# The value products of an attention pipeline in pairs, every second pass

## The reference

```
xl = layernorm(x)                      # 8 batches, 512 tokens, 128 features
q, k = xl @ W_qk ; v = xl @ W_v        # 8 heads, 64 features for q and k, 16 for v
dots = q k^T * 64**-0.5 + bias(head, clipped distance)
attn = softmax(dots) ; out = attn @ v
x = x + out @ W_out + b_out
```

## Time and profile before

| what | value |
|---|---|
| time, median of 3 runs | 1154.55 us (1154.54 to 1154.6) |
| the profiled execution's own time | 1156.07 us |
| its span, first to last instruction | 1154.2 us |
| attention stage in it | about 604 to 1059 us |
| PE, DVE, ACT, POOL busy over the span | 90%, 78%, 71%, 45% |
| DMA packets' mean rate | 78 GB/s |

### The profile page before, as it was taken

One profiled execution on the slowest core, in us unless ns is written; L12 is line 12 of the kernel. 1 busy time (PEld: TensorE's weight loads), 2 busy tenths in 40 slices (PEclk: granted clock), 3 DMA queues, 4 the chain that ended last, 5 costly groups with the idle time before them and its releaser, 6 DMA issues. The chain is left out here.

```text
span 1154.2 us, 23485 instructions
## 1 busy us (share of the span) xinstructions
PE 1035.0 (90%) x7816; PEld 797.0 (69%) x7816; DVE 896.2 (78%) x1941; ACT 823.9 (71%) x1736; POOL 516.6 (45%) x322
## 2 busy tenths in 40 slices
PE   4876699999999999979968999999999999987997
PEld 3443578999899899759965555555555555546897
DVE  7798998888889889856646778787878787785565
ACT  3997998898898988636645666676766676651665
POOL 0288898898998989634530001010101010111354
PEclk9997699999999999999989999999999999998999
DMA  3001265555786686333322000000000000001331
GB/s 98 4 3 40 69 154 141 133 155 140 192 253 163 180 217 170 92 97 107 95 76 60 1 1 19 1 19 1 20 1 19 1 20 1 20 20 61 108 97 51
DMA packets 107782, 89.50 MB, mean 78 GB/s; under 512 B 35815, under 2 KB 85740, under 8 KB 107664
## 3 DMA queue, kind: packets, MB, share of 16 engines
q1 hardware_dynamic: 98784, 66.02, 22.1%
q0 software_dynamic: 5568, 12.66, 3.1%
q10 hardware_dynamic: 3312, 9.33, 2.7%
HBM read 71.49 MB, written 17.39 MB: 77 GB/s over the span
## 5 line engine op out<-in xcount | busy, mean ns | idle before, releaser
L1084 DVE TENSOR_TENSOR_SCAN h<-d_a,p_dbu 128x1024 f32<-128x1024 f32 x128 | 289.7, 2279 | 30.4 <-ACT d_a L828 26.3
L770 POOL TENSOR_TENSOR h<-h,c_rep 128x1024 f32<-128x1024 f32 x126 | 297.6, 2391 | 22.1 <-DVE h L1084 20.8
L1412 POOL DMA_INDIRECT expert_rows<-r_row,r_dest x60 | 59.4, 991 | 447.5 <-DVEq L1307 432.8
L828 ACT ACTIVATE d_a<-arena,a_exp 128x511 f32<-128x511 f32 x256 | 167.9, 710 | 13.5 <-DVE h L1084 13.3
L2131 DVE CUSTOM_DVE_ANT_0 arena<-at_p_scores,arena 128x512 f32<-128x512 f32 x256 | 161.3, 686 | 19.0 <-PE at_p_scores L1934 17.2
L2140 DVE COPY at_probs_T<-at_p_probs_T 128x512 f32<-128x512 f32 x128 | 88.0, 687 | 72.8 <-PE at_p_probs_T L1942 72.1
L976 PE MATMUL p_y_T<-ident,h 128*128 128x128 f32 x1024 | 132.5, 273 | 1.2 <-DVE h L1139 1.1
L2047 ACT ACTIVATE at_probs<-arena,at_min 128x512 f32<-128x512 f32 x145 | 98.2, 712 | 47.0 <-DVE at_min L2131 47.0
L820 ACT ACTIVATE b_du_T<-arena,b_T 128x256 f32<-128x256 f32 x304 | 128.7, 495 | 0.0
L1934 PE MATMUL at_p_scores<-arena,at_q_T 64*128 64x512 f32 x512 | 127.2, 615 | 0.9 <-DVE arena L2123 0.9
L976 PEld LDWEIGHTS p_y_T<-ident,h 128*128 128x128 f32 x1024 | 115.9, 142 | 1.7 <-DVE h L1139 1.7
(11 more groups left out here) (272 smaller groups left out, 1767.6 us busy)
## 6 DMA issues: line engine op xcount, KB each, us to landing
c_rep<-c_rows SPq DMA_DIRECT2D x128, 256.0 KB
diag_b<-diag_rows SPq DMA_DIRECT2D x52, 256.0 KB
f_row<-expert_rows SPq DMA_DIRECT2D x78, 129.0 KB, 2.2
arena<-in_w_all ACTq DMA_DIRECT2D x8, 578.0 KB
arena<-bias_by_distance ACTq DMA_DIRECT2D x8, 448.0 KB
x_tok<-in_x SPq DMA_DIRECT2D x4, 512.0 KB, 5.7
x_tok<-x_between SPq DMA_DIRECT2D x8, 256.0 KB, 2.7
diag_rows<-diag_b SPq DMA_DIRECT2D x4, 256.0 KB, 3.0
```

The lines of the kernel that those rows point to most:

```text
L770: nc.gpsimd.tensor_tensor(h_at(n), h_at(n), cc, ALU.mult).then_inc(prod_done, 1)
L828: nc.scalar.activation(da[:, s % 2, ch, 1:], delta[:, one(b), ch, 1:].squeeze(1), ACT.Exp, scale=a_exp[:, ch, s:s + 1]).then_inc(da_ready, 1)
L1084: nc.vector.tensor_tensor_scan(h_at(n).rearrange("p c t -> p (c t)"), da[:, s % 2, :, :].rearrange("p c t -> p (c t)"), p_dbu[:, s % 2, :, ...
```

## The change

1. `values`: instead of one half group in each pass n >= 2, every odd pass n >= 3 makes both halves (`values(n-3)`, `values(n-2)`), and even passes make none.
2. V moves from slot A to slot B of pass 7, on PE and on ACT.
3. DVE: the part 0 of `norm(b, 0)` moves from ahead of the takes to between them in pass 5, part 1 to pass 6, part 2 to pass 7; in passes 6 and 7 `take(4n)` goes ahead of the fourth `bias`; `add_bias` moves behind the takes of pass 7.
4. Start: four dummy products fewer; the first two score products wait for q0 and k0 alone, the other two for q1 and k1.
5. End: the last group of values goes to a bank of `psc`, and normalising, output product and addition are made in two halves of 256 columns; the first half is normalised behind the takes of the last pass. Dummy products between: 2 instead of 9.

```
-        AT_A = {0: "X", 1: "k0", 2: "k1", 3: "q2", 4: "R", 5: "q3", 7: "V"}
-        AT_B = {0: "q0", 1: "q1", 2: "O", 3: "k2", 4: "L", 5: "N", 6: "k3"}
+        AT_A = {0: "X", 1: "k0", 2: "k1", 3: "q2", 4: "R", 5: "q3"}
+        AT_B = {0: "q0", 1: "q1", 2: "O", 3: "k2", 4: "L", 5: "N", 6: "k3", 7: "V"}
...
             def quad(n):
                 b, part = divmod(n, QUADS)
-                if part == 0:
-                    pe.wait_ge(proj_taken, taken(b, "q1" if b == 0 else "k1"))
-                    if b == 0:
-                        pe.wait_ge(first_k, 2)
+                if part == 0 and b > 0:
+                    pe.wait_ge(proj_taken, taken(b, "k1"))
...
                 for g in range(4 * n, 4 * n + 4):
...
+                    if g in (0, 2):
+                        pe.wait_ge(proj_taken, taken(0, "q0" if g == 0 else "q1"))
+                        pe.wait_ge(first_k, g // 2 + 1)
...
-            k.keep_busy(pot, 6)
+            k.keep_busy(pot, 2)
...
-                if n >= 2:
+                if n >= 3 and n % 2:
+                    values(n - 3)
                     values(n - 2)
...
+            def last_output(half):
+                pe.wait_ge(last_norm, 4 * half + 4)
+                for j in range(TPB // 2):
+                    at_t = (half * TPB // 2 + j) * P
+                    for gr in range(NG):
+                        mm = nc.tensor.matmul(last_out[half][:, j * P:(j + 1) * P], onT[gr][:, at_t:at_t + P],
+                                              w_o[:, gr, :], start=gr == 0, stop=gr == NG - 1)
+                mm.then_inc(o_half, 1)
+
+            pe.wait_ge(biased, ALL)
             for i in range(B * QUADS - 2, B * QUADS):
                 values(i)
-            pe.wait_ge(biased, ALL)
-            k.keep_busy(psc[:, 0, :], 9)
-            slot(B, "O")
+            use_bank(added, B)
+            pe.wait_ge(normed, B * NG - 1)
+            last_output(0)
+            k.keep_busy(psc[:, 0, :], 2)
+            last_output(1)
...
+            def last_normed(half):
...
+                dve.wait_ge(valued, 2 * n + 1 + half)
...
+                V.transpose(o_tok.rearrange("p n e -> p (n e)")[:, cols], last_sums[half]).then_inc(last_norm, 1)
...
-                elif part == 5:
-                    norm(b, 0, 0)
...
                 elif part == 5:
+                    norm(b, 0, 0)
+                elif part == 6:
                     norm(b, 0, 1)
-                elif part == 6:
+                elif part == 7:
                     norm(b, 0, 2)
-                elif part == 7 and b + 2 < B:
-                    add_bias(b + 2)
...
+                elif part == 7 and b + 2 < B:
+                    add_bias(b + 2)
+                elif part == 7 and b == B - 1:
+                    last_normed(0)
...
-                if n + 1 < B * QUADS:
-                    for g in range(4 * n + 4, 4 * n + 8):
+                more = n + 1 < B * QUADS
+                if more:
+                    for g in range(4 * n + 4, 4 * n + 7):
                         bias(g)
+                if part in (6, 7):
+                    take(4 * n)
+                if more:
+                    bias(4 * n + 7)
                 ahead_of_takes(b, part)
-                take(4 * n)
+                if part not in (6, 7):
+                    take(4 * n)
...
-            norm(B - 1, 1, 0, 1, 2)
-            add(B - 1)
+            last_normed(1)
+            last_add(0)
+            last_add(1)
```

More of the change, by code:

```diff
@@ L1807, in attention @@
         turned_taken = [S("turned_taken0"), S("turned_taken1")]
+        last_norm, o_half, half_added = S("last_norm"), S("o_half"), S("half_added")
         norm_step, normed, o_done, added = S("norm_step"), S("normed"), S("o_done"), S("added")
@@ L1825, in attention @@
         rt.veps, rt.rstd, rt.rstd_ready, rt.rstd_from = veps[:, 1, :], rstd[:, 1, :], rstd_ready, 3
+        LAST_VALUES = B * ST // VS - 1
+        HALF = T // 2
+        last_sums = [pot[:, 0:HALF], psc[:, 2, 0:HALF]]
+        last_out = [pmm[:, 0:HALF], psc[:, 1, 0:HALF]]
         LOGITS_READ, RANKS_READ = 12, 21
@@ L1959, in values @@
                     for q in range(HG):
-                        mm = nc.tensor.matmul(pot[32 * q:32 * q + 32, it * P:(it + 2) * P],
+                        dst = pot[32 * q:32 * q + 32, it * P:(it + 2) * P]
+                        if vg == LAST_VALUES:
+                            dst = psc[32 * q:32 * q + 32, 2, 0:HALF]
+                        mm = nc.tensor.matmul(dst,
                                               vv[b % 2][:, j, hd0 + q, :], prT[:, vg % 2, q, j, :],
@@ L2160, in norm, with last_add @@
                     V.transpose(onT[gr], o_norm).then_inc(normed, 1)
+            def last_normed(half):
+                n = B * NG - 1
+                cols, blocks = slice(half * HALF, (half + 1) * HALF), slice(half * HALF // 32, (half + 1) * HALF // 32)
+                dve.wait_ge(valued, 2 * n + 1 + half)
+                dve.wait_ge(norm_step, 2 * n)
+                V.transpose(o_tok.rearrange("p n e -> p (n e)")[:, cols], last_sums[half]).then_inc(last_norm, 1)
+                dve.wait_ge(last_norm, 4 * half + 1)
+                V.reciprocal(rden[:, blocks], o_tok[:, blocks, DV]).then_inc(last_norm, 1)
+                dve.wait_ge(last_norm, 4 * half + 2)
+                dve.wait_ge(normed, n)
+                V.tensor_tensor(o_normed[:, blocks, :], o_tok[:, blocks, :],
+                                rden[:, blocks].unsqueeze(2).to_broadcast([P, HALF // 32, 32]),
+                                ALU.mult).then_inc(last_norm, 1)
+                dve.wait_ge(last_norm, 4 * half + 3)
+                dve.wait_ge(o_done, B - 1)
+                V.transpose(onT[1][:, cols], o_norm[:, cols]).then_inc(last_norm, 1)
+            def last_add(half):
+                dve.wait_ge(o_half, half + 1)
+                dve.wait_ge(x_biased, B)
+                at_j = (B - 1) * TPB + half * TPB // 2
+                xb = k.x[:, at_j:at_j + TPB // 2, :]
+                V.tensor_tensor(xb, last_out[half].rearrange("p (j e) -> p j e", j=TPB // 2), xb,
+                                ALU.add).then_inc(added if half else half_added, 1)
             def add(b):
@@ L2228, in _ @@
             plan.make_pad(dve)
-            norm(B - 1, 1, 0, 1, 2)
-            add(B - 1)
+            last_normed(1)
+            last_add(0)
+            last_add(1)
+            dve.wait_ge(half_added, 1)
             route(B - 1, *range(0, 12))
```

## The result

| | before | after |
|---|---|---|
| median, us | 1154.57 (4 runs, 1154.54 to 1154.85) | 1166.47 (4 runs, 1165.53 to 1166.87) |
| ratio | 1 | 1.0107, 95% interval 1.0093 to 1.0122 |
| profiled execution: time, span, mean granted clock | 1156.07, 1154.2, 0.975 | 1166.5, 1164.5, 0.967 |

The kernel is 1.0 to 1.1% slower: the medians lie 11.9 us apart, which is 1.03%, and the ratio on record, which is not the quotient of the medians, is 1.0107. Forecast were 1156.8 us, 2.2 more than before, and a range that ended at 1163.0. The sign was right, the size was not.

A forecast was written before the change was run, and what follows sets the result against it. PE was taken to bound odd passes and a bias, exps and copy chain the even ones; 5.6 + 1.3 + 0.6 - 1.8 - 2.1 - 1.4 = +2.2 on 1154.55 us gave 1156.8, range 1154.0 to 1163.0.

The forecast's parts named there:

- rival C: Even passes leave PE idle 1 us or more, so the clock falls, 3 to 5 us each; chance 0.03.
- what stands outside the stage: Ahead of and behind the attention stage: forecast at 0 us in the sum.
- Odd passes bound by PE, even ones by bias, three exps and the copy of slot A: Passes 1, 3, 5, 7 change by +0.68, +0.62, +0.69, +0.29 us; passes 0, 2, 4, 6 by 0, -0.33, 0, -0.84.
- 0.86 for the second half group, not 1.00: In odd passes the joined second half of values adds 0.86 us, as one drain between groups goes.
- Pass 6, the early signal: In pass 6 PE's first two turns signal before the late stretch: 5.51 us (-0.84), or 6.35 (0) if held.
- Batch 7, start and end: Batch 7 -1.8 us; start of the stage -1.4 (bounds -0.4 and -1.5); end -2.1 (bounds -0 and -2.7).
- the 0.8 that I expected of its pass 6: Pass 6 of batch 7, which has no projections, gains 0.8 us, within that batch's estimate of -1.8.
- batches 1 to 5: The pass changes sum to +1.11 us for each of these five batches, +5.6 in all.
- the prediction's own sign of being wrong: Wrong if the granted clock falls within the stage, pass 0 comes under 6.2 us, or odd passes pass 7.7.
- The bound for "can tell" (0.2%): This kernel's measurement was taken to tell differences of about 0.2%, 2.3 us.

The follow-up runs named there:

- e4: The kernel before without the first half group of each pair of values, queries scaled by 0.01: 1157.34 us, against 1155.24 for before.
- e3: The kernel before, unchanged, run again on chip 1: 1155.58 us, ratio 1.0001.
- e11: The changed kernel with four dummy products ahead of slot B in pass 4 alone: 1160.89 us, ratio 1.0019 to the kernel before.
- e14: The changed kernel, unchanged, run again on chip 4: 1163.07 us, ratio 1.0072 to the kernel before.
- e2: The kernel before with only the start and end edits of the change: 1152.19 us, ratio 0.9975.
- e6: The changed kernel with one half group of values in every pass n >= 2 again, all other edits kept: 1151.39 us, ratio 0.9909 to before.
- e10: The kernel before with the router's sends of batches 0 to 5 held to run beside pass 0 of the next batch: 1161.83 us, ratio 1.0016.
- e12: The kernel of e6 with the router's sends held as in e10: 1152.15 us, ratio 0.9933 to the kernel before.
- e13: The changed kernel with values paired only in pass 7, none in pass 6, one half group in passes 0 to 5: 1149.18 us, ratio 0.9954 to before.
- e5: The changed kernel with eight dummy products ahead of slot B in passes 0 and 4 of each batch (not the first): 1167.88 us, ratio 1.0053 to before.
- e7: The changed kernel, unchanged, run again on chip 2: 1163.48 us, ratio 1.0007 to the kernel before.

## Why the prediction was wrong

Two terms that the sum had at nothing failed: the clock inside the stage (rival C, chance 0.03) took 3.29 us, and what stands outside the stage took 4.01 + 0.53 us in the compared execution (points 5 and 6). The mechanism of the passes held. Point by point:

1. *Odd passes bound by PE, even ones by bias, three exps and the copy of slot A.* Right, and shown by every trace of the change: where the clock held, the pass lengths came out within 0.1 us on four chips. e4 shows the even passes' half of it without any pairing.
2. *0.86 for the second half group, not 1.00.* Right: the odd passes carry it (7.52 forecast as 7.53). The 0.14 saved is nothing beside the 0.6 to 0.7 that passes 1, 3 and 5 lose each.
3. *Pass 6, the early signal.* Right, and worth 0.87 a batch against a before with late signals, 0.40 against one without. The size of the term changes with the chip or the execution, which the rows could not tell: before's pass 6 is 6.35, 5.89, 6.34 and 5.88 in its four profiles (the first comparison, chips 1, 3 and 4). The prediction's rule that signals due about 1.3 us or more behind the first send are seen late was read from one execution of before; in pass 6 of e3, with the same distances, nothing was late.
4. *Batch 7, start and end.* Batch 7's passes up to the last scores gave 36.72 - 37.59 = -0.87 without the clock (e11 against before); the 0.8 that I expected of its pass 6 falls by these landmarks into the end, which gave -2.61. Together -3.48, forecast -1.8 - 2.1 = -3.9. The start gave -0.71 in the first pair and -1.34 in e14 for -1.4. All of it, with the clock falls in the passes and what lies outside the stage taken out, is 10.33 - 3.29 - 4.01 - 0.53 = +2.5 us; the forecast was +2.2, and e11 measured +1.8. That it comes so near is partly luck: batches 1 to 5 cost 0.6 less than forecast and the start saved 0.7 less.
5. *"Rival C, the clock ... I give it little."* This is the step that failed within the stage, and the prediction's own sign of being wrong, a fall of the clock within it, came. I argued from pass 0 of batch 0, which held 1.00 with PE busy 5.35 of 6.37. Pass 4, just as empty in the table (5.33 of 6.49), is another thing: it is mostly transposes and small router products. In all six profiles of kernels without values in pass 4, and without a fill, low stretches lie at the end of pass 4 or in pass 5, one to five each; in no profile of before, e2, e6, e10, e12, e13, e5 or e11 does one. e5 and e11 differ from after by the fill alone, so the evidence is that the fall comes from what PE does not do in pass 4; it rests on one profile of each, and the falls without a fill are themselves irregular. One fall costs 1.5 to 1.7 us, not the 3 to 5 us that I had for it. The Trainium skill (TensorE: Matmul & The Clock Gate, "A second HAM failure mode: psum-queue depth-cycling") says of another kernel that the clock goes back and forth where the PE idles briefly and often between groups of matmuls; these runs agree in kind, but the clock fell about two of the eight passes 4 in the first profile, and about one of them in e7.
6. *The sum against one execution's time.* The other 4.01 us lay ahead of the stage, and 0.53 behind it. I took what is not changed to cost nothing, and in the mean it does: the sign of that term turned round on chip 4, and over all profiles x is loaded at 603.9 in the four of before and at 603.0 in the three of after. But one comparison carries it, and no bound of mine held it. The bound for "can tell" (0.2%) was too small likewise: before itself took 1154.6, 1155.2, 1163.2, 1159.1 and 1155.0 us in five comparisons, and after against before gave 1.0107, 1.0007 and 1.0072, or +11.9, +0.3 and +8.1 us between the medians. Their mean, +6.7, is near the +2.5 and 3.3 of point 4 and the clock together.

Open: why the copy on DVE took 4.71 us, and why all four runs of after in the first comparison were slow; how an indirect send holds back a signal of PE; and why pass 4 lets the clock fall and pass 0 does not. That pass 0 has a 512 column projection in its second slot is not the answer by itself, for pass 0 of batch 7 has no projection, makes PE wait 1.43 us where pass 4 of batches 1 to 7 makes it wait 1.15, and the clock held there in every profile. Pass 4 of batch 0, which has no router products, is as empty (PE busy 4.00 of 5.43) and never saw a fall either. Pass 0 of batch 7 in the first profile of the changed kernel:

```profile
1003.30:1008.74 5.44, 4.01 (x26) 2.40 (x25) 3.87 (x11) 3.97 (x7) 0.00 (x0) 1.00 0.01 2
```

## What to carry to other kernels

Cut a pipeline into its passes and find the limit of each before joining work: joining saves its small overhead once, but where another chain sets every second pass, the work taken out there buys nothing and all of it is paid in the passes that PE sets. Where PE must wait anyway, a few dummy products sized below the wait can hold the clock: with four it held at no cost in the one profile taken, and eight lengthened the pass. Work can be moved so that no awaited signal falls beside a known disturbance, as e13 does with PE's signals and the sends, but compare it on one chip with leaving the pair out. And compare the same two programs on more than one chip before believing a difference of about 1% or less.

## What was unexpected in the hardware

- The delay of PE's signals beside GpSimd's indirect sends: 0.45 us or nothing in pass 6 of one and the same program, in four profiles from four comparisons; 0 to 0.9 us in pass 7 within one execution of e6; about 1.5 us in pass 0 when the sends were moved there.
- Low clock stretches of 3.4 us behind a pass in which PE is 82% busy, each worth about 1.6 us: at the start of pass 5 of batch 7 in all three profiles of the changed kernel (1033.9, 1027.5 and 1030.0 us), and at the end of pass 4 of batch 1 in two of them. Pass 0 of batch 7, with PE 74% busy, never saw a fall.
- A DVE copy of 128x8 that took 2.34 to 2.42 us in fifteen profiles and 4.71 in two; in these two PE waited 4.02 instead of 1.7 us behind it and the clock fell, and 3.5 us were lost.
- A program unchanged from chip to chip differs by up to 8.6 us in its median (1154.6 and 1163.2), and two profiles of it differ by 5.4 us before the attention stage begins. On chip 1 two programs that are alike up to there reach it at 599.73 and 606.74 us.
